# An accumulating transfer on GpSimd's queue in place of GpSimd additions, in an attention and expert kernel

## The reference, cut to what matters

```python
x = x + attention(layernorm(x))
xt = layernorm(x)                                  # 4096 tokens x 256
scores = softmax(xt @ gate_w.T)
_, idx = top_k(scores + gate_bias, 2)              # two of eight experts for each token
weights = take_along_axis(scores, idx)
for e in range(8):
    gate_e = sum(where(idx == e, weights, 0), axis=1)
    y += gate_e[:, None] * ((silu(xt @ w1[e].T) * (xt @ w3[e].T)) @ w2[e].T)
z = (silu(xt @ sw1.T) * (xt @ sw3.T)) @ sw2.T      # shared expert
return x + y + z
```

## Time and profile before

| | |
|---|---|
| median of 3 runs | 622.0 us (621.9 to 622.91) |
| the profiled execution's own time | 621.86 us |
| its span | 620.1 us |
| TensorE, VectorE, ScalarE, GpSimd busy | 552.9, 441.1, 329.1, 291.3 us |
| last scatter of the slot loop starts | 569.9 us |
| DMA moved in the whole span | 63.03 MB |

### The profile page before, as it was taken

One profiled execution on the slowest core, in us unless ns is written; L12 is line 12 of the kernel. 1 busy time (PEld: TensorE's weight loads), 2 busy tenths in 40 slices (PEclk: granted clock), 3 DMA queues, 4 the chain that ended last, 5 costly groups with the idle time before them and its releaser, 6 DMA issues.

```text
span 620.1 us, 11503 instructions
## 1 busy us (share of the span) xinstructions
PE 552.9 (89%) x3468; PEld 480.1 (77%) x3468; DVE 441.1 (71%) x1202; ACT 329.1 (53%) x684; POOL 291.3 (47%) x593
## 2 busy tenths in 40 slices
PE   5869899977989969819999998999999999998874
PEld 4856799876589965508888886888888888887764
DVE  7949998594987756686767644666666666664895
ACT  3548997265998616414454432555555555554221
POOL 4047500206730016017767661466666766665690
PEclk9979899997989988958999999999999999999998
DMA  8999000000000039002222222233333333331994
GB/s 259 325 305 45 2 1 2 2 0 1 1 2 1 1 99 403 9 17 97 87 79 96 88 95 57 71 108 106 104 104 105 105 106 104 106 101 61 336 335 142
DMA packets 57129, 63.03 MB, mean 102 GB/s; under 512 B 14736, under 2 KB 50448, under 8 KB 57072
## 3 DMA queue, kind: packets, MB, share of 16 engines
q1 hardware_dynamic: 49216, 43.75, 24.8%
q0 software_dynamic: 6480, 17.90, 8.2%
q10 hardware_dynamic: 1376, 0.66, 0.4%
HBM read 30.64 MB, written 31.65 MB: 100 GB/s over the span
## 4 chain that ended last, share of the span: by engine, by line
PE 55%; DVE 6%; issue 1%; ACT 1%; POOL 0%; DVEq 0%; POOLq 0%
PE bank L1314 16%; PE bank L1316 15%; PE bank L1315 15%; PE bank L1437 3%; PE bank L1453 2%; PE bank L1322 1%; PE bank L1366 1%; DVE h_lo L1244 1%; DVE XN L1088 1%; DVE X L1227 0%; PE bank L1339 0%; DVE mv L1085 0%; DVE X L1217 0%; DVE hf L1236 0%; DVE XT_lo L1126 0%
## 5 line engine op out<-in xcount | busy, mean ns | idle before, releaser
L970 POOL DMA_INDIRECT token_out<-YS,to_row x71 | 71.7, 1010 | 54.0 <-DVE back L1281 49.8
L934 POOL DMA_INDIRECT slots_in<-X,slot x64 | 66.3, 1036 | 60.0 <-DVE slot L1201 30.4
L676 PE MATMUL a_bank<-VO,E_hi 128*128 128x258 f32 x272 | 78.5, 289 | 3.5 <-issue 1.8
L680 PE MATMUL a_bank<-VO,E_lo 128*128 128x258 f32 x272 | 78.5, 288 | 0.0
L678 PE MATMUL a_bank<-VO,E_hi 128*128 128x256 f32 x272 | 78.2, 288 | 0.0
L1270 DVE TENSOR_TENSOR hr<-bank,sr 128x256 f32<-128x256 f32 x71 | 30.1, 424 | 60.9 <-ACT sr L1047 60.9
L1314 PE MATMUL bank<-W_hi,XST_hi 128*128 x142 | 62.4, 439 | 0.5 <-DVE XST_lo L1286 0.5
L1047 ACT ACTIVATE sr<-bank 128x256 f32<-128x256 f32 x71 | 27.2, 383 | 64.7 <-PE bank L1316 64.7
L1021 ACT ACTIVATE h_hi<-hf 128x512 fp32r<-128x512 f32 x32 | 20.2, 632 | 73.1 <-DVE hf L1236 73.1
L1316 PE MATMUL bank<-W_hi,XST_lo 128*128 x142 | 57.1, 402 | 0.0
L1315 PE MATMUL bank<-W_lo,XST_hi 128*128 x142 | 56.8, 400 | 0.0
(11 more groups left out here) (247 smaller groups left out, 1675.3 us busy)
## 6 DMA issues: line engine op xcount, KB each, us to landing
XS<-slots_in SPq DMA_DIRECT2D x71, 131.0 KB, 2.0
slots_in<-blank SPq DMA_DIRECT2D x7, 1179.0 KB, 14.9
YG<-token_out SPq DMA_DIRECT2D x16, 512.0 KB, 8.8
W_raw<-in_wT_dram SPq DMA_DIRECT2D x8, 768.0 KB, 13.6
X<-in_x_dram SPq DMA_DIRECT2D x8, 512.0 KB, 8.4
out_dram<-X SPq DMA_DIRECT2D x32, 128.0 KB, 1.9
token_out<-YS,to_row POOLq DMA_INDIRECT x71, 2.5
slots_in<-blank SPq DMA_DIRECT2D x1, 1048.0 KB, 14.3
```

The lines of the kernel that those rows point to most:

```text
L676: pe.matmul(O_ps[Q % 2][j][:, 0:D + 2], E_hi[:, n % NE, cols], VO[:, kt, 0:D + 2], start=(kt == 0), stop=False)
L680: mm = pe.matmul(O_ps[Q % 2][j][:, 0:D + 2], E_lo[:, n % NE, cols], VO[:, kt, 0:D + 2], start=False, stop=(kt == qt))
L934: pool.indirect_dma_start(out=xs, out_offset=bass.IndirectOffsetOnAxis(ap=slot[k][:, t:t + 1], axis=0), in_=X[:, t, :], in_offset=None).th ...
L970: pool.indirect_dma_start(out=ys, out_offset=bass.IndirectOffsetOnAxis(ap=to_row[:, i:i + 1], axis=0), in_=YS[:, i % NYS, :], in_offset=No ...
```

## The change

YG holds one result for each token instead of two. SP loads only the first results, eight loads of 512 KB. GpSimd, when group g's load has landed, issues a transfer that reads the second results of the group from memory and adds them onto YG (`accum_op=ALU.add`); it does no additions. Each group has a semaphore of its own, s_yy[g], which the transfer raises when it has landed, and VectorE waits for it once for each group, ahead of both halves. The freed part of YG goes into the padding W_rest.

```diff
--- before.py
+++ after.py
@@ -756,8 +756,8 @@
                 pass
             with nc.sbuf_tensor("W_lo", [P, KC, NX, 3 * D], f32r) as W_lo:
                 pass
-        YG = sb("YG", [P, NT, TOPK, D])
-        sb("W_rest", [P, 2 * KC * NX * 3 * D - NT * TOPK * D])
+        YG = sb("YG", [P, NT, D])
+        sb("W_rest", [P, 2 * KC * NX * 3 * D - NT * D])
 
         with ExitStack() as first:
             def early(name, shape, dt=f32):
@@ -846,7 +846,7 @@
         s_meta = sem("f_meta")
         s_mt = sem("f_mt")
         s_y = sem("f_y")
-        s_yy = sem("f_yy")
+        s_yy = [sem(f"f_yy{g}") for g in range(NG)]
         s_out = sem("f_out")
 
 
@@ -890,9 +890,7 @@
             for v in range(NYS):
                 sp.wait_ge(s_yst[v], rows_back(v))
             for g in range(NG):
-                for k in range(TOPK):
-                    sp.dma_start(YG[:, g * GT:(g + 1) * GT, k, :],
-                                 ys_p[:, k * NT + g * GT:k * NT + (g + 1) * GT, :]).then_inc(s_yg[g], 16)
+                sp.dma_start(YG[:, g * GT:(g + 1) * GT, :], ys_p[:, g * GT:(g + 1) * GT, :]).then_inc(s_yg[g], 16)
             for g in range(NG):
                 for t in range(g * GT, g * GT + GT):
                     sp.wait_ge(s_y, t + 1)
@@ -970,11 +968,9 @@
                 pool.indirect_dma_start(out=ys, out_offset=bass.IndirectOffsetOnAxis(ap=to_row[:, i:i + 1], axis=0),
                                         in_=YS[:, i % NYS, :], in_offset=None).then_inc(s_yst[i % NYS], 16)
             for g in range(NG):
-                pool.wait_ge(s_yg[g], 16 * TOPK)
-                for h in range(0, GT, 2):
-                    tiles = slice(g * GT + h, g * GT + h + 2)
-                    pool.tensor_tensor(YG[:, tiles, 0, :], YG[:, tiles, 0, :], YG[:, tiles, 1, :], ALU.add)\
-                        .then_inc(s_yy, 1)
+                pool.wait_ge(s_yg[g], 16)
+                pool.dma_start(YG[:, g * GT:(g + 1) * GT, :], ys_p[:, NT + g * GT:NT + (g + 1) * GT, :],
+                               accum_op=ALU.add).then_inc(s_yy[g], 16)
 
         @block.scalar
         def _(act):
@@ -1211,10 +1207,10 @@
             def add_routed(g):
 
                 dve.wait_ge(s_zf, 2 * g + 2)
+                dve.wait_ge(s_yy[g], 16)
                 for h in range(0, GT, 2):
                     tiles = slice(g * GT + h, g * GT + h + 2)
-                    dve.wait_ge(s_yy, g * 2 + h // 2 + 1)
-                    dve.tensor_tensor(X[:, tiles, 0:D], X[:, tiles, 0:D], YG[:, tiles, 0, :], ALU.add)\
+                    dve.tensor_tensor(X[:, tiles, 0:D], X[:, tiles, 0:D], YG[:, tiles, :], ALU.add)\
                        .then_inc(s_y, 2)
 
             def add_shared(G, z):
```

## The result

The changed kernel takes 626.88 us (median of 4 runs, 626.23 to 627.76), against 621.95 us for the kernel before beside it: a ratio of 1.0075 with a 95% interval of 1.0059 to 1.0091. It is slower, by 3 to 5 us. The prediction was 626.5, with a range from 615.7 to 641.

What follows compares the result with a forecast made beforehand. The bound moves from TensorE and VectorE to the DMA engines: their work ends at 621.9, plus 1.8 to the span's end and 1.1 idle is 624.8, time 626.6, predicted as 626.5; range 615.7 to 641.

Steps and rivals of the forecast that it cites:

- What bound the kernel: Tail: TensorE busiest, waiting on VectorE, which GpSimd's sixteen additions slow; some 6.2 us are waits and what follows them.
- The prize: Tail: removing GpSimd's additions lets TensorE finish its outputs at 604.5 instead of 610.75, 6.2 us, time 615.7.
- The price of an accumulating packet: DMA engines: two fetches, 90 ns per 1 KB piece, so a = 2.9 us of 16 engines for each 512 KB transfer.
- The sum of the work: DMA engines from 574.7: loads 12.0, accumulates 23.2, stores 12.0 us, ending at 621.9; 47 us where it was 36.
- Two terms at the end: End of the tail: 1.1 us of idle engines and 1.8 us from the last bytes to the span's end.
- The waits, group by group: VectorE ahead of each group's additions: sum 0 on time, lateness growing to some 10 us at sum 7.
- the prediction's 584.4: Time by which sum 0 must be there to cost VectorE and TensorE nothing; each later one 4.2 us after.
- the foretold 10 us at the end: VectorE's wait for sum 7: some 10 us late, taking back the 6.2 us and 4 to 5 more.
- rival 1: DMA engines: an accumulate costs little more than a load, a = 1.5 to 2.2, time 615.7 to 618; chance 0.21.
- rival 2: DMA engines: a from 2.25 to 2.4, or whole-packet turns bring early sums on time; 621 to 623, chance 0.08.
- Fetch, fetch and write without overlap: DMA engines: three steps in turn, a = 4.5 us, work 60 us, ending at 639.4; chance 0.12.
- rival 4: GpSimd: writing descriptors becomes the bound, up to 8 us a transfer; 648, or 632 at 6 us; chance 0.09.

Runs made afterwards that it cites:

- e7: Kernel before without GpSimd's sixteen additions; both loads stay, VectorE adds only the first result, the second is left out: 617.29 us, ratio 0.9881.
- e4: Changed kernel, but SP issues each next load only when the previous group's accumulating transfer has landed, so each runs alone: 683.12 us, one run.
- e1: Changed kernel with GpSimd's eight transfers copying the second results over the first instead of adding them: 618.49 us, ratio 0.9898.
- e2: Changed kernel accumulating only two of each group's four tiles, half of the second results left out: 618.37 us, ratio 0.9929.
- e5: Changed kernel with the additions of groups 5 and 6 moved behind the last h_lo on VectorE: 625.19 us, ratio 1.0047 to the kernel before.
- e12: The changed kernel again, unedited, against the kernel before on one chip: 627.58 us, ratio 1.0052.
- e10: Changed kernel with SP holding at most two loads in flight: 628.55 us, one run.
- e6: Kernel before with the additions of two groups moved behind the last h_lo: 622.48 us, ratio 0.9998.

## Why the prediction was right

**What bound the kernel.** Right, and shown by e7: without GpSimd's additions VectorE's rows are short and the tail loses 5.2 us. The prize was put at 6.2; what was missed is that TensorE's clock was at 0.50 in the last outputs, behind its last wait.

**The price of an accumulating packet.** Taken as two fetches, 90 ns and a = 2.9 us. Measured 83 to 85 ns alone (e4) and 83 to 85 beside plain packets, a = 2.7. The Trainium skill's page Collectives: The Full Stack (The bandwidth ceiling) has a ratio of 1.93 between a collective that copies and one that reduces, which it puts down to two reads. Here it is 83 / 45 = 1.84, so rule and measurement agree within 5%. (The prediction's 1.5 x 1.93 is 2.9 and not 2.8; 45 ns x 32 x 1.93 is 2.8.) That two reads are the mechanism is argued from the ratio; no run here separates them from the addition. What is shown is that the price is the engines', since e1 and e2 lower it and the tail follows.

**The sum of the work.** Forecast to end 49.4 us into the tail (621.9 - 572.5), the span 2.9 later, a tail of 52.3. Measured 51.5. With 2.7 for 2.9 the work is 1.6 us less. Two terms at the end were off and cancel: in the trace the engines are full until 620.7, all but idle until 622.4, and move the last bytes until 624.4, 0.8 us before the end of the span. That is some 2.2 us of idle engines where 1.1 was taken, and 0.8 behind the last bytes where 1.8 was.

**The waits, group by group.** The mechanism was right and one step of the working was not. It gave the two queues even shares of the engines' time, so 5.8 to 6 us between sums at first. They have even shares of packets, so the accumulates get 85 of 130 ns and a sum comes each 32 x 130 = 4.2 us: the additions start at 588.60, 592.96, 598.23, 602.48, 606.78, 611.02 and 615.24 (one step of 5.3 is not explained). That is the 4.2 us of a chunk. Against the times that would cost nothing (the prediction's 584.4 and each 4.2 us after, plus 1.2 for the later start of this tail) VectorE is late by 3.0, 3.2, 4.2, 4.3, 4.4 and 4.4 us for groups 0 to 5: the wait does not grow from sum to sum, as the prediction had as a sign. Only where no further chunk stands between two sums does it fall back, to 7.3 us for group 6 and 10.1 for group 7 (this one with TensorE's last wait and slow clock in it), so the foretold 10 us at the end came, with most of it in the last two steps. Against it, sum 0 was foretold 11.5 us into the tail and came at 14.9, because the first packet moved 5.0 us after the issue and not 1.5. Both errors together left the end about where it was, since the engines had plain work to do in the meantime (share 1.09 from 576 to 580 us).

**What was not foreseen.** TensorE's last wait grew to 6.30 us and its last twelve matmuls ran at the 1.2 GHz level. e5 shows what both cost the tail: 1.3 us. And 1.2 us of the difference between the two profiled spans was spread ahead of the tail. The prediction's 626.5 is thus nearer to 626.88 than its parts are, by luck: the tail was forecast 0.8 too long, which this spread covers. The growth in time was forecast at 4.5 us and measured at 4.9 and, in e12, at 3.5.

**The rivals.** An accumulate for little more than a load (rival 1) is refuted by e4; its result, 615.7 to 618, is about what e1 measures for plain copies, 618.49. Of rival 2 the mechanism came true, turns that go by packets and favour the accumulates, and its result did not: early sums were late all the same, by 3.0 us at sum 0, because the first packet was, and the time is above its 621 to 623. Fetch, fetch and write without overlap (4.5 us) is refuted by the same 83 ns. GpSimd as the bound (rival 4): it is held 1.28 us by each issue and has issued all eight by 597.7.

```profile
L972 POOL DMA_DIRECT2D YG<-token_out x8: 1279/1283/1410, 578.4 to 596.4; - x8
...
DMA to landing us min/median/max: 10.1/21.0/23.3
```

The eighth is issued at 596.4 and lands some 22 us later: it waits in the queue, not on GpSimd. The bounds by rows, 4 to 8 us of GpSimd for a transfer, were three to six times too high.

## What to carry to other kernels

An addition that moves into a transfer is not free: here an accumulating 1 KB packet costs the DMA engines as much as 1.84 plain ones, so first ask whether the engines have room for it until the last result is stored, and take it for no more than the part that fits. When two engines slow each other down, look whether the slower path is needed at all: VectorE alone could add both results of five or six of eight groups in its idle time, and this with three or two accumulating groups was 0.6 to 0.9% faster than the kernel before. Between the two queues of this kernel the turns were even in packets (2452 to 2450) and not in time, so the dear packets took 83 to 85 of each 130 ns.

## What the runs showed of the hardware

- Alone, an accumulating transfer of 512 KB in 1 KB pieces runs at 192 to 197 GB/s, 83 to 85 ns a packet (e4); plain loads at 349 to 355 GB/s, 45 ns (before).
- The software and the hardware queue moved equal numbers of packets over 20 us, 2452 to 2450 (changed kernel).
- The first packet of a transfer issued from GpSimd came 2.1 us after its issue with idle engines (e4), 5.0 us with SP's queue full (changed kernel), 3.2 us with two loads in flight (e10).
- TensorE's granted clock was at 0.50, the 1.2 GHz level, for the last outputs after 6.30 us without a matmul (changed kernel). After 2.42 us it was 0.50 in e7, but in the kernel before still 1.00 from 613.0 to 614.5 us, and lower only for the last two matmuls; after 0.80 us it was 1.00 (e5, e6).
- Plain copies on GpSimd's queue (e1) went in packets of 3.6 KB on average, where SP's loads of the same shape go in packets of 1 KB.
